# A wavelet, attention and ternary-weight layer on one core: preparation reordered, rotary partners on adjacent partitions, projection groups in another order

## What is computed

```python
# 1. tokens: three Haar analysis levels; nine softmax gates and one sigmoid
#    gate per image, each from a product of a whole band with a weight vector
w = softmax(stack([h, v, d]).reshape(B, -1) @ Wd + bd)     # per level
rec = idwt2(rec, h * w[:, 0], v * w[:, 1], d * w[:, 2])    # back to 256 x 256
# a class token is put in front: 257 tokens of 256 features
# 2. attention, 16 heads of 64, with layer norm ahead of it
q = q * cos + rotate_half(q) * sin        # partners are features i and i + 32
k = k * cos + rotate_half(k) * sin
scores = q @ k.T / sqrt(192) + alibi      # causal; softmax; times v; w_out; residual
# 3. gated MLP with ternary weights and activations quantised per token
wq = clip(round(w * scale), -1, 1) / scale       # scale = 1 / mean(abs(w))
h = h + bitlinear(silu(bitlinear(x, w_gate)) * bitlinear(x, w_up), w_down)
```

## Time and profile before

| | us |
|---|---|
| median of 3 runs | 1822.09 |
| lowest, highest | 1819.44, 1848.63 |
| the profiled execution's own time | 1818.61 |
| its span, first to last instruction | 1816.7 |
| PE busy in the span | 1678.3 (92%) |
| DVE, ACT, POOL busy | 1488.2, 1325.0, 1155.1 |
| mean granted PE clock | 0.958 of 2.4 GHz |

### The profile page before, as it was taken

How to read it: one execution, slowest core, us unless ns; L and a number is a source line. 1 busy time by engine, 2 the same in 40 slices (tenths; PEclk the granted TensorE clock), 3 DMA queues, 4 the chain that set the end, 5 groups by cost and what they waited for, 6 DMA issues and landing times.

```text
span 1816.7 us, 49299 instructions
## 1 busy us (share of the span) xinstructions
PE 1678.3 (92%) x16742; PEld 1283.4 (71%) x16742; DVE 1488.2 (82%) x4964; ACT 1325.0 (73%) x3808; POOL 1155.1 (64%) x1291
## 2 busy tenths in 40 slices
PE   1855799999999999999999999999999999999975
PEld 1743477777777777777777777777777777777752
DVE  1271589899988888888889998888888889999884
ACT  0111588888888888888878887888888888888862
POOL 0006767776777777777777777777777777777600
PEclk7856999999999999999999999999999999999996
DMA  8402222222222222222222222222222222222200
GB/s 240 168 1 58 53 54 54 58 57 61 60 58 65 66 66 61 58 60 58 57 52 66 60 60 59 66 66 65 58 58 60 57 58 55 66 59 52 57 7 12
DMA packets 98075, 113.76 MB, mean 63 GB/s; under 512 B 22721, under 2 KB 60066, under 8 KB 97570
## 3 DMA queue, kind: packets, MB, share of 16 engines
q1 hardware_dynamic: 97826, 110.61, 23.4%
HBM read 26.62 MB, written 8.42 MB: 19 GB/s over the span
## 4 chain that ended last, share of the span: by engine, by line
PE 82%; DVE 3%; POOL 2%; ACT 2%; issue 1%; DMA 1%; SPq 1%; DVEq 0%; POOLq 0%; ACTq 0%
PE bank L691 42%; PE bank L797 9%; PE bank L930 7%; PE bank L786 6%; PE bank L784 6%; PE bank L941 3%; PE bank L808 3%; PE bank L858 2%; PE bank L846 2%; PE bank L950 2%; PE bank L837 1%; DMA rot<-rq 1%; POOL arena L463 1%; POOL rot L459 1%; SPq L353 1%
## 5 line engine op out<-in xcount | busy, mean ns | idle before, releaser
L455 POOL TENSOR_TENSOR arena<-rq,cos 128x256 f32<-128x256 f32 (+1 forms) x384 | 344.4, 912 | 234.0 <-ACT rq L497 234.0
L506 ACT ACTIVATE arena<-arena,nm 128x129 f32<-128x129 f32 (+1 forms) x1024 | 455.7, 455 | 0.0
L459 POOL TENSOR_TENSOR rot<-rot,sin 128x512 f32<-128x512 f32 x256 | 326.2, 1274 | 150.2 <-DMA rot<-rq 149.1
L691 PE MATMUL bank<-xt_h,weights 128*128 128x256 f16 x2048 | 384.2, 276 | 9.3 <-ACT rq L497 6.5
L463 POOL TENSOR_TENSOR arena<-arena,rot 128x256 f32<-128x256 f32 (+1 forms) x384 | 332.0, 879 | 37.0 <-POOL rot L459 0.4
L497 ACT ACTIVATE rq<-bank,bqk 128x256 f32<-128x256 f32 x512 | 214.4, 471 | 175.0 <-PE bank L691 163.6
L1216 DVE CUSTOM_DVE_ANT_0 arena<-bank,bias 128x129 f32<-128x129 f32 (+1 forms) x1024 | 318.0, 352 | 27.1 <-issue 16.6
L1224 DVE TENSOR_TENSOR ptr_l<-bank,ptr_h 128x384 f16<-128x384 f32 x512 | 280.0, 552 | 34.8 <-ACT ptr_h L516 32.4
L516 ACT ACTIVATE ptr_h<-bank 128x384 f16<-128x384 f32 x512 | 249.1, 487 | 68.3 <-PE bank L691 43.7
L691 PE MATMUL bank<-xt_l,weights 128*128 128x256 f16 x1024 | 282.1, 275 | 0.0
L797 PE MATMUL bank<-eye,arena 128*128 128x128 f32 x1536 | 251.9, 276 | 9.1 <-DVE ptr_l L1224 4.7
(11 more groups left out here) (187 smaller groups left out, 3207.9 us busy)
## 6 DMA issues: line engine op xcount, KB each, us to landing
rot<-rq SPq DMA_DIRECT2D x1024, 64.0 KB, 2.0
arena<-in_x SPq DMA_DIRECT2D x4, 2048.0 KB, 15.1
xin<-in_x SPq DMA_DIRECT2D x32, 256.0 KB, 3.0
hr<-hr SPq DMA_DIRECT2D x32, 256.0 KB, 2.3
out<-h SPq DMA_DIRECT2D x64, 128.0 KB, 2.1
arena<-in_L_attn_w_qkv SPq DMA_DIRECT2D x2, 1536.0 KB, 6.5
arena<-in_L_attn_w_out SPq DMA_DIRECT2D x1, 1024.0 KB, 9.6
arena<-in_L_ffn_w_gate SPq DMA_DIRECT2D x1, 1024.0 KB, 6.9
```

The costliest lines, as they stand in the source:

```text
L455: ins = pool.tensor_tensor(dst, rq[:, g % 2, :, cols], cos[:, cols].unsqueeze(1).broadcast_to([P, 2, cols.stop - cols.start]), ALU.mult)
L459: pool.tensor_tensor(r, r, sin[:, :].unsqueeze(1).broadcast_to([P, 2, SIDE]), ALU.mult).then_inc(t2_ready, 1)
L506: act.activation(cols, cols, ACT.Exp, bias=nm[:, t, h:h + 1], scale=-1.0, accum_out=rs[:, t, h:h + 1]).then_inc(e_done, 1)
L691: ins = pe.matmul(dst, lhs[l], rhs[r], start=start and n == 0, stop=stop and n == len(parts) - 1)
```

## The change

Four things are edited.

1. Constants: `eye`, `rel`, `mask`, `avg` and the class token are loaded ahead of the pixels and DVE waits for these five alone. `cos`, `sin` and the small biases go behind the weights, on semaphores of their own (`late_in`, `bias_in`).
2. Weights: `w_down` is loaded right behind the pixels into free space in `weights`, `w_gate` and `w_up` after quarter 1, image 0 behind them, the attention weights after quarters 2 and 3. DVE's bias tables, row patterns, absolute sums and the ternary passes of two weights go ahead of its wait for `z_done` 4; each ternary weight has a tile of its own. The last ternary weight's passes stand between the gate instructions. PE waits for the absolute sums between quarters 3 and 4 of the pixel sums.
3. Image 0: the operators of image 0 are made alone, those of images 1 to 16 and 17 to 31 later. POOL makes image 0's sums ahead of time. `prep_done` is gone; finer semaphores stand in its place, and image 0's calls up to `project(0, 0)` are written out with the rest of the preparation between them. `add_bias(0)` waits for `ob_copied`.
4. Rotation: features are laid out so that partners i and i + 32 are on adjacent partitions (written through a stride of two in the weights' split, and by strided transfers for `cos`, `sin` and the biases). A group's exchange is two transfers of 64 partitions each. L455 and L463 become one instruction for key groups too. The groups go in the order `GROUPS`, a query group and its key group as a pair, and `scores(c, j)` waits for the pairs that it needs.

```diff
+GROUPS = [0, 4, 1, 5, 2, 6, 3, 7]
...
-        wv_h, wv_l = half_view(4096, 1024, KC), half_view(5120, 1024, KC)
-        wo_h, wo_l = half_view(6144, 1024, PAIRS), half_view(7168, 1024, PAIRS)
+        wv_l, wv_h = half_view(4096, 1024, KC), half_view(7168, 1024, KC)
+        wo_h, wo_l = half_view(5120, 1024, PAIRS), half_view(6144, 1024, PAIRS)
...
+            for dst, q in ((wqk[:, k, 0:n], 0), (wqk[:, k, n:2 * n], 1)):
+                dst = dst.rearrange("p (h i two) -> p two h i", h=HEADS, two=2)
+                for turn in range(2):
+                    yield dst[:, turn], raw[:, k, :, q * DH + turn * 32:q * DH + (turn + 1) * 32]
+            yield wv[:, k, :].rearrange("p (h d) -> p h d", h=HEADS), raw[:, k, :, 2 * DH:3 * DH]
...
-            for dst, src in ((rel, c_rel), (mask, c_mask), (eye[:, :], c_eye)):
+            for dst, src in ((eye[:, :], c_eye), (rel, c_rel), (mask, c_mask), (avg[:, :, :], c_avg)):
                 sp.dma_start(dst, src).then_inc(const_in, 16)
             for q in range(4):
...
+            sp.dma_start(rawd.rearrange("p (m n) -> p m n", n=INNER), w_down.rearrange("(m p) n -> p m n", p=P)).then_inc(ff_in, 16)
+            sp.wait_ge(z_done, 1)
+            for r, w in ((rawg, w_gate), (rawu, w_up)):
...
             load_x(0)
-            sp.wait_ge(prep_done, 1)
+            for k, b in enumerate((bd1, bd2, bd3)):
...
+            sp.wait_ge(z_done, 2)
+            sp.dma_start(raw[:, 0], w_qkv[0:P]).then_inc(raw_in[0], 16)
...
+            sp.wait_ge(z_done, 3)
+            sp.dma_start(raw[:, 1], w_qkv[P:2 * P]).then_inc(raw_in[1], 16)
+            sp.dma_start(rawo, w_out.rearrange("(j a) d m -> (a d) j m", a=2)).then_inc(rawo_in, 16)
+            sp.dma_start(bo_row, b_out.unsqueeze(0)).then_inc(late_in, 16)
+            for dst, src in ((cos, c_cos), (sin, c_sin)):
+                for two in range(2):
+                    for turn in range(2):
+                        at = two * DH + turn * 32
+                        sp.dma_start(dst[two * DH + turn:(two + 1) * DH:2, :], src[at:at + 32, :]).then_inc(late_in, 16)
...
-                for q in range(4):
-                    src = (q ^ 1) * 32
-                    sp.dma_start(rot[q * 32:q * 32 + 32, g % 2], rq[src:src + 32, g % 2]).then_inc(rot_done[g % 2], 16)
+                for q in range(2):
+                    sp.dma_start(rot[q::2, g % 2], rq[1 - q::2, g % 2]).then_inc(rot_done[g % 2], 16)
```

POOL, ahead of its loop (`first_operators` is L424 to L433 for image 0, with the pixel sums first):

```diff
+            first_operators()
+            pool.wait_ge(late_in, 16 * 13)
```

PE, at the end of the pixel sums' loop and after it (`turn_weights` is L769 for one weight, `cls_part` a part of L744, `out_bias` a part of L752):

```diff
                 ins.then_inc(z_done, 1)
+                if q == 2:
+                    pe.wait_ge(fill_done, 5)
+                    pe.wait_ge(abs_ready, 3)
+                    pe.matmul(psum[1][:, 0:3], ones[:, :], wsc[:, 0:3], start=True, stop=True).then_inc(cls_turned, 1)
             pe.wait_ge(zm_ready, 1)
...
+            pe.wait_ge(mean_ready, 1)
+            turn_weights(0)
+            turn_weights(1)
+            pe.wait_ge(xct_ready, 1)
+            for k in range(KC):
+                pe.wait_ge(raw_in[k], 16)
+            cls_part(psum[4], (0, 1), range(0, 4))
+            pe.wait_ge(spread_gates, 1)
+            pe.matmul(psum[6][:, 0:IMAGES * FACTORS], ones[0:IMAGES, :], spread_out, start=True, stop=True).then_inc(bcast_ready, 1)
+            cls_part(psum[4], (0, 1), range(4, PAIRS))
+            turn_weights(2)
...
-                if j == 0:
-                    pe.wait_ge(qk_done, 8 * c + 8)
+                if j % 2 == 0:
+                    pe.wait_ge(qk_done, 8 * c + j + 2)
...
+            synthesise(0)
+            coarse(0)
+            pe.wait_ge(turned_copied, 4)
+            cls_part(psum[3], (2,), range(PAIRS))
+            turn_input(0)
+            pe.wait_ge(rawo_in, 16)
+            pe.wait_ge(late_in, 16 * 13)
+            pe.wait_ge(vcls_ready, 1)
+            out_bias(range(0, 4))
+            project(0, 0)
+            out_bias(range(4, PAIRS))
+            pe.matmul(psum[2][:, 0:SIDE], ones[0:1, :], bo_row, start=False, stop=True).then_inc(ob_ready, 1)
```

DVE, ahead of its loop, below the gate maps, bias tables and `row_patterns` (`ternary(k, part)` is one pass over weight k, `weights_split` L1161, `image_operators(i, n)` L1105 and L1108 for n images):

```diff
+            dve.wait_ge(ff_in, 16 * 3)
+            for k, w in enumerate((rawg, rawu, rawd)):
+                dve.tensor_reduce(wsc[:, k:k + 1], w, AX.X, ALU.add, apply_absolute_value=True).then_inc(abs_ready, 1)
+            dve.wait_ge(cls_turned, 2)
...
+            for k in range(2):
+                for part in range(3):
+                    ternary(k, part)
             dve.wait_ge(z_done, 4)
...
+            ternary(2, 0)
+            dve.wait_ge(late_in, 16 * 13)
             softmax_inputs()
+            ternary(2, 1)
             image_factors()
             spread_factors()
+            ternary(2, 2)
+            dve.wait_ge(bcast_ready, 1)
+            link(dve.tensor_copy(fac[:, :], psum[6][:, 0:IMAGES * FACTORS]))
+            image_operators(0, 1)
             for k in range(KC):
+                weights_split(k, range(4))
+            dve.wait_ge(cls_kv, 2)
+            dve.wait_ge(bias_in, 16 * 6)
...
+            image_out(0)
+            image_stats(0)
+            dve.wait_ge(cls_kv, 3)
+            tt(vcls, psum[3][:, 2 * PAIRS:3 * PAIRS], bv[:, :], ALU.add).then_inc(vcls_ready, 1)
+            normalise_image(0)
+            dve.wait_ge(ops_ready, 1)
+            image_operators(1, 16)
+            input_lo(0)
+            prep_chain.settle()
+            dve.tensor_copy(gs[:, 40:41], magic[:, :]).then_inc(w_split, 1)
+            for k in range(KC):
+                weights_split(k, (4,))
+            dve.wait_ge(w_hi, 11)
+            stt(wo_l[:, :, :], rawo, WSCALE, wo_h[:, :, :], ALU.mult, ALU.subtract).then_inc(wo_split, 1)
...
+            dve.tensor_copy(ob[:, :], psum[2][:, 0:SIDE]).then_inc(ob_copied, 1)
+            dve.wait_ge(ops_ready, 2)
+            image_operators(17, 15)
```

More of the change, by code:

```diff
@@ L829, in turn_input @@
             def turn_input(a):
-                if not image(a):
+                if not image(a) or begun and a == 0:
                     return
@@ L861, in project @@
             def project(b, g):
[L862 removed]
+                if not image(b) or begun and (b, g) == (0, 0):
                     return
+                if g == 0 and b == 0:
+                    pe.wait_ge(w_split, 1)
                 if g == 0:
```

310 lines of the change are left out of this document (154 added, 156 removed).

## The result

| | before | after |
|---|---|---|
| median of the runs beside each other, us | 1820.76 (1817.64 to 1848.63, 4 runs) | 1753.49 (1752.32 to 1755.07, 4 runs) |
| profiled execution, us | 1818.61 | 1752.32 |
| its span, us; mean granted clock | 1816.7; 0.958 | 1750.5; 0.976 |

The ratio is 0.9639, with a 95% interval of 0.9623 to 0.9656: faster by 3.6%. The ratio is formed from fast runs alone, without the 1848.63 us of before. The forecast was 1764 with a range of 1751 to 1784, so the time lies 10.5 us under it, near the lower end. The spans differ by 66.2 us where 56.4 were forecast.

The account below looks back on a forecast made before the run. PE was taken to bound the middle, leaving the time until PE saturates; 53.6 (first sine product) + 2.2 + 0.6 (rotation) = 56.4 us off 1818.6 gave 1762.2, stated as 1764 us, range 1751 to 1784.

Parts of the forecast that it names:

- Part 1: Constants and gate maps: DVE starts near 12 us, pixel sums at 23, quarters 1 to 3 end at 32, 39, 46.
- Part 2: Weights loaded during pixel sums: landing at 45 us, PE idle 6 us, quarter 4 from 52.4 to 61.5.
- the rule that the prediction drew from the Trainium skill: Pixel sums' quarter 4: PE gaps lower the clock and bursts start slowly, so 9.1 us, without it 7.0.
- Part 3: Gates and image 0: gates done at 67.5 us, first projection at 90.7, 54.5 us earlier; first sine product at 100.3.
- I take no wait: DVE before the gates: late_in lands by 61 us, before 63.3, so no wait; price of the other end 7.7 us.
- The second added wait is the costliest: POOL's add_bias(0) waits for ob, all POOL work behind it; constant copied by 97.7 us, sine product at 100.3.
- Part 4: Rotation: two issues for four, 1.1 us less a group; 2.2 us from early waits, 0.6 from single key-group instructions.
- they cost nothing, since PE has no gap: Middle of the run: POOL's waits, about 12 us an image, are free, so the period stays at 49 us.
- Rivals A: Loads or hand-offs set the pace: gates about 8 us later, gain 44 us, 1776 us; chance 0.22.
- B: Start moves but leftovers on DVE or a colder PE lose half the gain: 28 us, 1792 us; chance 0.08.
- C: Slower: the interleaved exchange is slow and the loop becomes POOL's; 1855 us at that point; chance 0.04.
- Rival D: More gained: clock stays up, loads come at once, PE not behind at gates; 6 us more, 1757; chance within forecast's 0.66.

Follow-up runs that it names:

- The part alone: Kernel before the change with only the small constants moved ahead of the pixels in SyncE's queue: 1795.16 us, ratio 0.9875.
- a kernel whose first sine product is 2.2 us later: Changed kernel with GpSimd forming image 1's row operators ahead of image 0's rotations, not behind the third: 1748.78 us, ratio 0.9622.

## Why the prediction was right, and where it was not

**The prediction was right in sign and size**, and the range held. The forecast gain was 56.4 us, the measured one 66.2. The first sine product came 4.2 us earlier than forecast, and the middle gave some 7 us where nothing was forecast. Both errors have one sign, and the time is 2.5 us inside the lower bound: that it stayed inside is in part luck. The step from the sum's 1762.2 to the 1764 of the forecast is also loose, since the 3.5 us named for it give 1765.7.

**Part 1, constants.** Sums forecast at 23, measured at 22.77; VectorE's start at 12, measured at 11.67. Three quarters ended at 45.9, forecast 46. The part alone is worth 23.4 us.

**Part 2, weights.** Landing forecast at 45, measured 44.26. Quarter 4 forecast 52.4 to 61.5, measured 51.57 to 60.03, 8.46 us for the 9.1. The pause cost nothing, as forecast. What made it so is the weights' landing: VectorE's chain begins there and ends last. The clock in these stretches of the changed kernel, to be read with the earlier trace rows (stretch, us, busy time of PE with its matmuls, clock, DMA share, GB/s):

```profile
46.00:51.50 5.50, 0.42 (x2) 0.94 0.75 219
51.50:55.00 3.50, 3.50 (x21) 0.61 0.73 170
55.00:60.00 5.00, 5.00 (x47) 1.00 1.00 380
60.00:67.00 7.00, 4.13 (x99) 1.00 0.19 59
...
69.00:72.00 3.00, 3.00 (x60) 0.50 0.00 0
...
102.00:110.00 8.00, 1.46 (x6) 0.50 0.18 66
```

At the end of the 5.15 us pause the clock fell to its lower level (1.2 GHz), and from 55 on it was at the upper one (2.4); the 0.94 and 0.61 of the first two rows are means over both levels. Here the rule that the prediction drew from the Trainium skill, page "TensorE: Matmul & The Clock Gate", section "HAM oscillation — how this bites in real kernels", and the trace agree: 8.46 us is nearer to the 9.1 with the rule than to the 7.0 without. In the kernel with `avg` behind the pixels the quarter took 7.18 us, after a pause of 1.29.

**Part 3, gates and image 0.** "I take no wait" for `late_in` was off by 1.38 us, within its bound of 7.7. The spread gates were there at 67.3, forecast 67.5. The sum was too long at PE: "it turns two weights (3.5 at the lower clock, after 62.2) and does a third of the class token products, a third of 10.4, to 69.2". These ran at the upper level, 2.05 us for the products, and were over by 64.8. So the spread waited for the gates alone, at 67.39 for 69.2, and took 1.20 for 1.7, and the coarse sum ended 2.5 us earlier than the 80.8; `synthesise` and `coarse` themselves took the 4.5 forecast. From the start of normalising to the first projection it took 5.3 us for 6.2. The strided writes of the splits cost nothing: the eight half-size ones take 5.0 us in the kernel with the operators first, where 4.9 were taken.

```profile
78.11 5.00 DVE L1192 SCALAR_TENSOR_TENSOR weights<-arena,weights 128x512 f16<-128x512 f32 x8
```

The 6.09 us of the changed kernel have another source: one split, beside GpSimd's row operator at 69.95 to 71.51, takes 1.78 us, the others 0.71 to 0.73 each. First projection 87.07 for 90.7.

**"The second added wait is the costliest"** has the right row and the wrong weight. The copy of the constant began at 91.77, not at 97.2: 3.6 us of this from the first projection, and most of the rest since PE's products from there on ran at the upper level (0.95 between 88 and 92 us). The bias then took 2.61 us for 1.3, and the first sine product came at 96.07 for 100.3. But moving the wait gave 0.2 us, and a kernel whose first sine product is 2.2 us later is 4.7 us faster. The instant chosen as the measure of the start was not what set it.

**Part 4, rotation.** The two waits of image 0 and 1 shrank from 2.70 and 2.67 to 1.76 and 1.41, 2.2 us together as summed. That they reach the total isn't shown: the lead grew by 2.2 from image 0 to image 2 in one execution and shrank by 1.3 in the other. That the pairs and the finer wait release nothing was right. The key groups' single instruction shows in GpSimd's busy time and not in the kernel's.

**The step that failed** is the first one: "they cost nothing, since PE has no gap" and "the middle of the run should stay at its period". It was read off one window of 49 us. Over 1200 us PE had lost little (1197.58 busy, against 1199.81 after), yet an image took 0.26 us more; the kernel before, at 49.32 us, was itself over the 49.2 that the prediction named as a sign of being wrong. Four issues in place of two bring the loss back. One way is seen: 4 of some 195 exchanges between 400 and 1600 us hold ScalarE, and what stands behind in ScalarE's order is wanted by PE. That is 1.5 of 6.2 us, and in the kernel with the old rotation the loss is there almost without it. Idle PE as a whole accounts for 2.2 us: the rest is hidden in a busy time whose ends are modelled, and stays open.

The ledger, by experiments: constants 23.4 us; exchange 5.4 to 9.5; of the remaining 33 to 37, the weights under the sums and the preparation around image 0, no single edit was run. Rivals A, B and C didn't come about: the loads landed as the sum had them, half the gain was not lost, and 128 KB with a partition step of two land in 2.0 us. Rival D (1757) was nearest, for its reason, the clock, and for one that it hadn't.

## What to carry to other kernels

An engine that is busy 99.8% of the time in a window can still be held up a little in every iteration, so compare the instants of one instruction per iteration, over many, before a part of a change is booked at nothing. Ask of each wait on an engine with slack what stands behind it on that engine, and who wants that. Constants that open a chain belong ahead of bulk loads even in a queue that is never empty, and in a pipeline's first iterations look at what the busiest engine waits for in its fixed order, not only at the first instant at which the next engine may begin. When an edit moves an instant by one microsecond, measure it from the last instant that the edit can't have touched: two executions of one kernel differ by half of that.

## What the runs showed of the hardware

A GpSimd instruction that meets a VectorE instruction with two SBUF inputs waited it out in the cases below. In the kernel with the operators first the row operator takes 2.74 us beside a product of VectorE, and the bias addition, with none beside it, 1.26:

```profile
71.06 2.74 POOL L441 TENSOR_TENSOR rowop<-ops,avg 128x512 f32<-128x512 f32 x1 [24.67 <-DVE ops L1174]
...
95.78 1.26 POOL L500 TENSOR_TENSOR hr<-hh,ob 128x512 f32<-128x512 f32 x1 [9.59 <-DVE ob L1482]
```

```profile
70.93 1.76 DVE L1171 TENSOR_TENSOR arena<-fac,pats 128x1536 f32<-128x1536 f32 x1
```

VectorE's product ends at 72.69 and GpSimd's at 73.80, 1.1 us behind. The changed kernel's bias ends 1.1 us behind the product of 92.11 to 93.76, and the 3.00 us cosine product 1.1 us behind a split that ends at 90.51: each time nearly its whole own length of 1.26. Beside VectorE's reduction of 93.80 to 95.62, which reads one input, the cosine product of 94.85 took its 1.26. It goes the other way too: the split that meets the row operator takes 1.78 us, and ends 0.6 behind it.

The Trainium skill, page "GPSIMD Engine Reference", section "1. Specifications", says that GpSimd's SBUF interfaces contend with VectorE instructions that have two SBUF inputs; the trace agrees, with the sizes above. It explains why the cosine product moved ahead of the bias bought next to nothing: work pulled into that stretch stretches.

Matmuls of one column follow the clock too: 64 class products took 2.05 us at the upper level (a mean clock of 1.00 in their stretch) and 3.60 at the lower one (0.50).
